# Clustered 1x1 convolution on one core: the order of the first three units, and squares summed by fp32 products

## The reference

```
xn  = x / |x| ;  cn = centroids / |centroids|       # over the channels
idx = argmax_n (xn . cn)                            # the nearest centroid of each place
mean[n] = mean of the x of all places whose idx is n    # the image's own centroids
delta = mean[idx] - x
alpha = exp(-mean over channels of delta^2)
y   = x + alpha * delta
out = relu(W y + bias)
```

## Time and profile before

| | us |
|---|---|
| median of 3 runs (lowest, highest) | 459.74 (459.32, 461.93) |
| the profiled execution | 459.06 |
| its span, first to last instruction | 457.3 |
| TensorE busy | 423.6 (93% of the span) |
| VectorE busy | 292.1 (64%) |
| ScalarE busy | 243.7 (53%) |
| GpSimd busy | 206.1 (45%) |

### The profile page before, as it was taken

The page is one execution under the profiler, slowest core; times in us unless marked ns, Lnnn a source line. Parts: engine busy times, 40 slices in busy tenths (PEclk is TensorE's granted clock), DMA queues, the critical chain, the costliest instruction groups (busy, mean ns, idle before and its releaser), DMA issues.

```text
span 457.3 us, 5730 instructions
## 1 busy us (share of the span) xinstructions
PE 423.6 (93%) x2100; PEld 294.1 (64%) x2100; DVE 292.1 (64%) x386; ACT 243.7 (53%) x330; POOL 206.1 (45%) x102
## 2 busy tenths in 40 slices
PE   4965677699999999999999999999999999999997
PEld 3722344367767775777676775777586776777785
DVE  2444697394767495676777486758578476577740
ACT  5452334354674566555565466455465467466542
POOL 2000047063582585384574476276556458233440
PEclk9996788989999999999999999999999999999999
DMA  8991046979756857487937966585928402221133
GB/s 285 287 224 46 1 92 143 225 212 249 190 179 174 195 195 176 140 239 174 267 100 186 241 177 189 132 235 148 259 93 207 163 7 87 92 80 54 52 127 149
DMA packets 70927, 73.94 MB, mean 162 GB/s; under 512 B 2724, under 2 KB 45732, under 8 KB 70900
## 3 DMA queue, kind: packets, MB, share of 16 engines
q1 hardware_dynamic: 70900, 73.58, 58.4%
HBM read 48.40 MB, written 25.17 MB: 161 GB/s over the span
## 4 chain that ended last, share of the span: by engine, by line
PE 89%; DVE 5%; issue 3%; ACT 1%; DMA 1%; SPq 0%; ACTq 0%; DVEq 0%
PE main L751 19%; PE main L753 19%; PE main L752 19%; PE fa L668 10%; PE sump L709 9%; PE gat L732 5%; PE al L739 1%; PE fa L692 1%; DMA x<-x 1%; PE al L740 1%; PE fa L677 1%; DVE z L361 1%; DVE z L341 1%; DVE xt L286 1%; PE main L762 1%
## 5 line engine op out<-in xcount | busy, mean ns | idle before, releaser
L256 POOL TENSOR_TENSOR z<-z,x 128x1024 f32<-128x1024 f32 x43 | 101.7, 2386 | 221.2 <-DVE z L361 221.2
L751 PE MATMUL main<-yh,wh 128*128 128x512 f32 x376 | 153.9, 409 | 2.1 <-ACT o L512 2.1
L753 PE MATMUL main<-yh,wl 128*128 128x512 f32 x376 | 147.8, 393 | 0.0
L752 PE MATMUL main<-yl,wh 128*128 128x512 f32 x376 | 147.6, 392 | 0.0
L341 DVE TENSOR_TENSOR z<-gat,x 128x1024 f32<-128x1024 f32 x47 | 57.4, 1221 | 93.4 <-PE gat L732 93.4
L512 ACT ACTIVATE o<-main,bcol 128x512 f32<-128x512 f32 x96 | 65.9, 687 | 85.8 <-PE main L753 85.8
L263 POOL TENSOR_TENSOR yl<-z,yh 128x1024 fp32r<-128x1024 f32 x43 | 103.0, 2410 | 12.1 <-ACT yh L504 12.1
L751 PEld LDWEIGHTS main<-yh,wh 128*128 128x128 f32 x376 | 71.0, 189 | 23.6 <-issue 4.6
L753 PEld LDWEIGHTS main<-yh,wl 128*128 128x128 f32 x376 | 71.0, 189 | 16.0
L752 PEld LDWEIGHTS main<-yl,wh 128*128 128x128 f32 x376 | 71.2, 189 | 14.7
L504 ACT ACTIVATE yh<-z 128x1024 fp32r<-128x1024 f32 x48 | 50.5, 1051 | 17.2 <-POOL z L256 16.0
(11 more groups left out here) (99 smaller groups left out, 321.7 us busy)
## 6 DMA issues: line engine op xcount, KB each, us to landing
x<-x SPq DMA_DIRECT2D x24, 1024.0 KB, 5.6
out<-o SPq DMA_DIRECT2D x23, 1024.0 KB, 4.7
xs<-x SPq DMA_DIRECT2D x84, 256.0 KB, 5.9
o<-w SPq DMA_DIRECT2D x1, 1024.0 KB, 12.1
out<-o SPq DMA_DIRECT2D x4, 256.0 KB, 2.0
sq<-centroids SPq DMA_DIRECT2D x2, 80.0 KB
bcol<-bias SPq DMA_DIRECT2D x1, 2.0 KB, 11.5
```

Source lines behind the costliest of these rows:

```text
L256: pool.tensor_tensor(z, z, X[g // PARTS % 2][:, pair(h), span(g)], ALU.add).then_inc(y_pool, 1)
L751: t_.matmul(main[:, o % 2, :], WH[:, k, rows], YH[g % 2][:, k, :], start=(k == 0), stop=False)
L752: t_.matmul(main[:, o % 2, :], WH[:, k, rows], YL[g % 2][:, k, :], start=False, stop=False)
L753: last = t_.matmul(main[:, o % 2, :], WL[:, k, rows], YH[g % 2][:, k, :], start=False, stop=(k == KC - 1))
```

## The change

Units 0 and 1 (DIRECT = 2) no longer add their squares on VectorE. ScalarE writes all four blocks of squares into the output tiles OUT[0] and OUT[1], which are free then, and `sum_squares_direct` sums them over blocks and partitions by four fp32 products with the matrix of ones, each 128 x 512 with 128 weight columns, into `al` (unit 0) or a bank of `gat` (unit 1). Both halves of y of unit 0 are made by VectorE, both low halves by GpSimd (before: half 0 of each by VectorE, half 1 by GpSimd). The second halves of the gathers of units 0 and 1 go to `main`. The means of image 0 lie in `al` instead of `fa`, so that the similarities of image 1 wait for the copied one-hot matrix and no longer for G. The lists ahead of the loop are reordered on TensorE, VectorE and ScalarE: among it, image 1's argmax comes right behind the four deltas of units 0 and 1, its cluster sums stand between the convolution steps of unit 0, and the similarities of units 1 and 2 follow each other. Unit 0's third output block is convolved in two pieces. SP loads x of unit 4 before the blocks of unit 3 and x of unit 5 before the blocks of unit 4. The loop is the same but for the counts in waits, and `relu(0, 3)`, which has moved ahead of it.

The diff without context lines, cut to its core:

```
@@ -33,0 +34,2 @@
+DIRECT = 2
@@ -40 +42,6 @@
...
@@ -40 +42,6 @@
-def on_vector(g, h):
+def y_on_vector(g, h):
+    return g == 0 or (g >= TAIL and h == 1)
+def low_on_vector(g, h):
@@ -42 +49 @@
-    return (g == 0 and h == 0) or (g >= TAIL and h == 1)
+    return g >= TAIL and h == 1
...
@@ -49,2 +57,4 @@
-def made_by_pool(g, h):
-    return 2 * g + h + 1 - made_by_vector(g, h)
+def folded(g):
+    return max(0, g + 1 - DIRECT)
@@ -116 +126,6 @@
-        mean = fa[0:NK, 0, :]
+        def mean(b):
+    return al[0:NK, :] if b == 0 else fa[0:NK, 0, :]
+        def alpha(g):
+    return gat[:, 0, :] if g == 1 else al[:, :]
@@ -157 +172,6 @@
-    return main if (g, h) == (0, 1) else gat
+    return main if g < DIRECT and h == 1 else gat
+        def squares(g, h):
+    if g < DIRECT:
+        return OUT[g][:, pair(h), :]
+    return SQ[:, :, :] if h == 0 else gat[:, :, :]
...
@@ -203,3 +225,6 @@
-    for g in range(PARTS, 2 * PARTS):
-        load_x(g)
-        load_xs(g)
+    load_x(3)
+    load_x(4)
+    load_xs(3)
+    load_x(5)
+    load_xs(4)
+    load_xs(5)
...
@@ -345 +370 @@
-        upper = banks(g, 1)
+        upper = squares(g, 1)
@@ -349 +374 @@
-        dve.wait_ge(pair_done, 2 * g + 2)
+        dve.wait_ge(pair_done, 2 * folded(g))
@@ -354 +379 @@
-        dve.wait_ge(sh_done, g + 1)
+        dve.wait_ge(sh_done, folded(g))
@@ -361 +386 @@
-        v_.tensor_tensor(z, z, al[:, :].unsqueeze(1).to_broadcast([P, 2, UNIT]), ALU.mult
+        v_.tensor_tensor(z, z, alpha(g).unsqueeze(1).to_broadcast([P, 2, UNIT]), ALU.mult
...
@@ -408,0 +434 @@
+    transpose_half(3, 0)
@@ -412,7 +438,5 @@
-    delta(0, 0)
-    delta(0, 1)
-    add_squares(0)
-    delta(1, 0)
-    low_sum(0)
-    delta(1, 1)
-    transpose_half(3, 0)
+    transpose_half(3, 1)
+    for g in range(DIRECT):
+        delta(g, 0)
+        delta(g, 1)
+    argmax(1)
@@ -422,9 +446 @@
-    add_squares(1)
-    low_half(0, 0)
-    low_sum(1)
-    transpose_half(3, 1)
-    argmax(1)
-    delta(2, 0)
-    scale(1, 0)
-    scale(1, 1)
-    delta(2, 1)
+    y_half(0, 1)
@@ -433 +449,2 @@
-    add_squares(2)
+    scale(1, 0)
+    scale(1, 1)
@@ -435 +451,0 @@
-    low_sum(2)
@@ -436,0 +453,2 @@
+    delta(2, 0)
+    delta(2, 1)
@@ -438,0 +457 @@
+    add_squares(2)
@@ -439,0 +459 @@
+    low_sum(2)
@@ -487,4 +507,7 @@
-        if h == 0:
-            wait(act, s_done, g)
-        a_.activation(SQ[:, :, :] if h == 0 else banks(g, 1)[:, :, :], Z[g % 2][:, pair(h), :], ACT.Square
-              ).then_inc(sq_done, 1)
+        if g < DIRECT:
+            act.wait_ge(wT_ps, KC)
+            act.wait_ge(const_done, 7)
+        elif h == 0:
+            wait(act, s_done, folded(g - 1))
+        a_.activation(squares(g, h), Z[g % 2][:, pair(h), :], ACT.Square).then_inc(sq_done, 1)
...
@@ -499 +522 @@
-        a_.activation(al[:, :], al[:, :], ACT.Exp, scale=-1.0 / C).then_inc(exp_done, 1)
+        a_.activation(alpha(g), alpha(g), ACT.Exp, scale=-1.0 / C).then_inc(exp_done, 1)
...
@@ -566 +592,0 @@
-    keep_transposed(1, 1)
@@ -567,0 +594 @@
+    keep_transposed(1, 1)
@@ -570,6 +597,5 @@
-    for k in range(KC):
-        act.wait_ge(wT_ps, k + 1)
-        a_.activation(WH[:, k, :], wT(k), ACT.Copy).then_inc(wh_done, 1)
-        if k == 0:
-            copy_onehot(0)
-    evacuate_onehot(0)
+    high_weights(0)
+    high_weights(1)
+    copy_onehot(0)
+    high_weights(2)
+    high_weights(3)
@@ -576,0 +603 @@
+    evacuate_onehot(0)
@@ -579 +605,0 @@
@@ -580,0 +607 @@
+    copy_sims(4)
@@ -581,0 +609 @@
+    copy_sims(5)
@@ -583,2 +610,0 @@
-    high_sum(0)
-    copy_sims(4)
@@ -586 +611,0 @@
-    exp(0)
@@ -588 +613,3 @@
-    copy_sims(5)
+    exp(0)
+    copy_onehot(1)
+    exp(1)
@@ -590 +616,0 @@
-    high_sum(1)
@@ -592,4 +617,0 @@
-    exp(1)
-    copy_onehot(1)
-    square(2, 0)
-    square(2, 1)
@@ -599 +620,0 @@
-    high_sum(2)
@@ -601,2 +622 @@
-    relu(0, 2)
-    evacuate_onehot(1)
+    square(2, 0)
@@ -603,0 +624,2 @@
+    square(2, 1)
+    evacuate_onehot(1)
@@ -604,0 +627,3 @@
+    high_sum(2)
+    relu(0, 2)
+    relu(0, 3)
@@ -609 +634,2 @@
-        relu(g - 3, 3)
+        if g > PARTS:
+            relu(g - 3, 3)
@@ -657 +683,3 @@
-        wait(pe, g_ready, b)
+        if b == 1:
+            pe.wait_ge(ohT_done, 1)
+        wait(pe, g_ready, b if b > 1 else 0)
...
-        pe.wait_ge(ohT_done, b + 1)
+        if b > 0:
+            pe.wait_ge(ohT_done, b + 1)
@@ -719,2 +748,2 @@
-        t_.matmul(mean, rows, sumsH[:, :], start=True, stop=False)
-        t_.matmul(mean, rows, sumsL[:, :], start=False, stop=True).then_inc(cop_done, 1)
+        t_.matmul(mean(b), rows, sumsH[:, :], start=True, stop=False)
+        t_.matmul(mean(b), rows, sumsL[:, :], start=False, stop=True).then_inc(cop_done, 1)
@@ -726,3 +755,5 @@
-        if h == 0:
-            wait(pe, s_done, g)
-        elif banks(g, h) is gat:
+        if g == 0:
+            pe.wait_ge(wl_done, KC)
+        elif g < DIRECT:
+            pe.wait_ge(z_done, 2 * (g - 1) + h + 1)
+        elif h == 1:
@@ -729,0 +761,5 @@
+        elif g == DIRECT:
+            pe.wait_ge(za_done, 2 * g)
+        else:
+            pe.wait_ge(s_done, folded(g - 1))
@@ -737,2 +773,2 @@
-        pe.wait_ge(sh_done, g + 1)
-        pe.wait_ge(sl_done, g + 1)
+        pe.wait_ge(sh_done, folded(g))
+        pe.wait_ge(sl_done, folded(g))
@@ -742,5 +778 @@
-    def convolve(g, o):
-        if not 0 <= g < UNITS:
-            return
-        wait(pe, relu_done, KC * g + o - 1)
-        rows = slice(o * P, (o + 1) * P)
+    def sum_squares_direct(g):
...
+            if k % 2 == 0:
+        pe.wait_ge(sq_done, 2 * g + k // 2 + 1)
+            last = t_.matmul(alpha(g), ones[:, :].bitcast(F32), OUT[g][:, k, :],
+             start=(k == 0), stop=(k == KC - 1))
+        last.then_inc(one_done, 1)
+    def convolve(g, o, ks=range(KC)):
+        if ks[0] == 0:
+            wait(pe, relu_done, KC * g + o - 1)
+        rows = slice(o * P, (o + 1) * P)
+        for k in ks:
@@ -755 +798,2 @@
-        last.then_inc(main_done, 1)
+        if ks[-1] == KC - 1:
+            last.then_inc(main_done, 1)
@@ -771,0 +816,14 @@
+    def transpose_weights(k):
+        pe.wait_ge(w_in, 16)
+        pe.wait_ge(xe_act, 3 if k < 2 else 4)
+        for o in range(KC):
+            last = t_.transpose(wT(k)[:, o * P:(o + 1) * P], Wraw[:, o, k * P:(k + 1) * P], ident[:, :])
+        last.then_inc(wT_ps, 1)
+    def high_passes(ks):
+        for o in range(2):
+            for k in ks:
+        for weights in (WH, WL):
+            t_.matmul(main[:, o, :], weights[:, k, o * P:(o + 1) * P], YH[0][:, k, :],
+              start=(k == 0 and weights is WH), stop=False)
@@ -775,0 +834 @@
+    similarities(2)
@@ -776,0 +836 @@
+    transpose_sims(0)
@@ -778 +837,0 @@
-    similarities(2)
@@ -780 +838,0 @@
-    transpose_sims(0)
@@ -782,6 +840,2 @@
-    pe.wait_ge(w_in, 16)
-    for k in range(KC):
-        pe.wait_ge(xe_act, 3 if k < 2 else 4)
-        for o in range(KC):
-            last = t_.transpose(wT(k)[:, o * P:(o + 1) * P], Wraw[:, o, k * P:(k + 1) * P], ident[:, :])
-        last.then_inc(wT_ps, 1)
+    transpose_weights(0)
+    transpose_weights(1)
@@ -790 +844,2 @@
-    transpose_onehot(0)
+    transpose_weights(2)
+    transpose_weights(3)
@@ -792,0 +848 @@
+    transpose_onehot(0)
@@ -795 +851,2 @@
-    pe.wait_ge(wl_done, KC)
+    similarities(3)
+    similarities(4)
@@ -798 +855 @@
-    similarities(3)
+    similarities(5)
@@ -801,3 +857,0 @@
-    similarities(4)
-    sum_squares(0)
-    similarities(5)
@@ -805,8 +859,3 @@
-    def high_passes(ks):
-        for o in range(2):
-            for k in ks:
-        for weights in (WH, WL):
-            t_.matmul(main[:, o, :], weights[:, k, o * P:(o + 1) * P], YH[0][:, k, :],
-              start=(k == 0 and weights is WH), stop=False)
+    sum_squares_direct(0)
+    sum_squares_direct(1)
+    sum_clusters(1, 0)
@@ -815,2 +863,0 @@
-    sum_squares(1)
-    gather(2, 0)
@@ -819 +866 @@
-    gather(2, 1)
+    sum_clusters(1, 1)
@@ -827,4 +874,3 @@
-    convolve(0, 2)
-    sum_squares(2)
-    for u in range(PARTS):
-        sum_clusters(1, u)
+    gather(2, 0)
+    sum_clusters(1, 2)
+    gather(2, 1)
@@ -832 +878 @@
-    convolve(0, 3)
+    convolve(0, 2, range(0, 2))
@@ -833,0 +880,3 @@
+    convolve(0, 2, range(2, KC))
+    convolve(0, 3)
+    sum_squares(2)
```

More of the change, by code:

```diff
@@ L325, in rest_of_mean @@
                 dve.wait_ge(mean_step, 2 * b + 2)
-                v_.scalar_tensor_tensor(out=mean, in0=part[:, :], scalar=below2[:, :], in1=mean,
+                v_.scalar_tensor_tensor(out=mean(b), in0=part[:, :], scalar=below2[:, :], in1=mean(b),
                                         op0=ALU.mult, op1=ALU.add).then_inc(rest_step, 1)
                 dve.wait_ge(rest_step, 2 * b + 1)
-                v_.tensor_copy(part[:, :], mean).then_inc(rest_step, 1)
+                v_.tensor_copy(part[:, :], mean(b)).then_inc(rest_step, 1)
             def parts_of_mean(b):
@@ L333, in parts_of_mean @@
```

(56 more changed lines are left out.)

66 lines of the change are left out of this document (27 added, 39 removed).

## The result

The changed kernel takes 435.56 us (median of 4 runs, 435.03 to 436.3), the kernel before 460.84 beside it: ratio 0.9449, 95% interval 0.9419 to 0.948. The forecast was 437.5 us, with a chance of 0.65 for 432.5 to 440. The profiled execution has a span of 433.4 us, TensorE busy 420.2 of them, and a mean granted clock of 1.00 (before 0.973).

What follows compares the result with a forecast made beforehand. TensorE was taken to bound the loop, so only an earlier loop start pays: 459.06 us, minus 20.2 for the start and 1.7 for the clock patch, gives 437.2, stated as 437.5 (432.5 to 440, chance 0.65).

Steps and rivals of the forecast that it cites:

- What bounds the kernel: TensorE fills the loop over units 3 to 23, busy 343.72 of 344.00 us; only an earlier loop start pays.
- Parts 1 and 2: Start to argmax 1: means scaled at 31.0 us, first gather 34.7, argmax 1 at 40.5, 21.9 us earlier.
- Part 3: Squares of units 0 and 1: eight fp32 products at 0.88 us make 7.0 us, mostly covered; 0.44 the lower bound.
- Part 4: Argmax 1 to the loop: GpSimd's chain decides; TensorE gap 2.8 us from 60.5; gather of unit 3 at 68.75.
- Part 5: Clock: 1.7 us charged behind TensorE's gap at 60.5, loop start 70.4; 1.76 us saved behind the old gap.
- low end: 432.5 us: 0.44 us products (0.8), no clock loss at 60.5 (1.7) and 2 for overlap not seen.
- (b): Rival: only the eight direct products meet the low clock, 7 us more up to unit 1's exponential; 444, chance 0.14.
- (a): Rival, slower: the lower clock stays before the loop, which starts at about 98 us; 466.5, chance 0.03.
- Part 6: Transfers: unit 5's x there by 33 us, wanted at 35.6; units 6 and 7 by 68; nothing on the path.
- (c): Rival: gain given back by handovers before the loop or unit 7's late x, 3 to 6 us; 441, 0.17 with (d).
- (d): Rival: unit 5's x lands late, so argmax 1 moves less; about 2 us at 38, 439; chance 0.17 with (c).

## Why the prediction was right, and where it was off

**What bounds the kernel** held: the loop stayed as dense as it was, and the gain is the earlier start and the slow patch at its beginning.

**Parts 1 and 2** came out within 0.2 us: scaling of the means at 31.01 (forecast 31.0), first gather 34.65 (34.7), first delta 35.67 (35.85), argmax 1 at 40.42 (40.5). Undoing the bank (7.2 us) and the load order (1.8 us) shows what they rest on. Argmax 1 at 40.42 is not itself what the gain hangs on: with it at 48.50 only 2.0 us are lost. What counts is that unit 0's y, and with it GpSimd, starts early.

**Part 3**, the price of a full-width fp32 product: eight records in 3.43 us (39.23 to 42.66), 0.86 us per product, the upper reading of the cluster sum's records and not the 0.44 us of their spacing. The rule of the Trainium skill (FP8 and Floating Point Precision, TensorE Precision Notes), four passes for true FP32, fits the trace: 0.86 us is 3.7 times the 0.23 us of a rounded product. What it was to cost was smaller still than reckoned: 0.8 us by the working, 0 by the run with rounded products, because GpSimd loses under VectorE's addition (0.50 us) what it wins by starting sooner (0.52 us).

**Part 4**: GpSimd's chain decides, as said (doubling one half moved the start by 2.37 us). Two of its sizes were off and cancel, which is luck: unit 0's high half starts at 46.79 instead of 47.25, and the two low halves last 5.33 us instead of 4.8, so GpSimd's first y half starts at 53.22 as against 53.1. The third did not cancel: ScalarE's one-hot copy is done at 62.83 instead of 63.3, since its operations overlap a little where they follow each other, and TensorE's gap is 2.0 us instead of 2.8. The start is at 68.11 against 68.75 before the clock's charge. That the distance from argmax 1 to G equals the old one was no argument, as the late argmax shows.

**Part 5** is the step that failed in size: 1.7 us were charged for a lower clock behind TensorE's gap, and none of the ten executions of the changed kernel shows it. It is most of what the forecast is too high by, 435.4 against a span of 433.4: 1.7 for the clock, 0.6 for part 4, less 0.3 in the loop's length. The forecast's low end took this in. Its high end is said to take in (b), but (b) at 444 lies outside the 440 beside it; the measurement is well under both. The rivals with a persistent low clock, (a) and (b), did not occur: TensorE had no idle time in the direct products, and the clock was 1.00. The kernel with VectorE's sums shows a clock of 0.50 from 45 to 57 us, so their mechanism is real in this stretch.

**Part 6** held for the new order; (c) and (d) did not occur.

## What to carry to other kernels

When a prologue is a chain over four engines, look for the idle time of the bottleneck engine and ask which buffer keeps ready work out of it: here one PSUM bank for the means, with the orders that it allows, was worth 7 us, and summing squares on the idle TensorE, at 0.86 us a product where a rounded one takes 0.23, up to 9. Such filler can count twice, as it also keeps up the engine's clock. Check too what an operation that waits holds back behind it in its engine's queue: that was 3 of the 9 us. To find which chain sets the end, double one operation on it: two distances that are equal before and after prove nothing.

## What the runs showed of the hardware

GpSimd's subtraction of two SBUF tiles (128 x 1024) lasts 2.36 us alone, 2.98 with 0.70 us of overlap with VectorE's addition of two SBUF tiles, and 3.48 with 1.22 us: about 0.9 us lost for each us of overlap, while the addition itself keeps its 1.23 us. The Trainium skill (SBUF — State Buffer, Who interferes with whom) says that a VectorE instruction with two SBUF inputs contends with a GpSimd instruction that reads SBUF; the rows agree. Here VectorE's addition had started first (47.19 and 47.69), and the loss is on GpSimd's side. In the kernel before it is the other way round:

```profile
57.24 2.38 POOL L256 TENSOR_TENSOR z<-z,x 128x1024 f32<-128x1024 f32 x1 [54.17 <-DVE z L361]
```

GpSimd keeps its 2.38 us there, and VectorE's subtraction that starts at 59.00, 0.62 us before GpSimd is done, lasts 1.70 us instead of the 1.23 of the same line alone.

The same kernel can keep its clock in one execution and lose it in another: with 3.4 us of idle at 61 us one of six had a mean clock of 1.00, the others 0.992 to 0.996. The length of this one gap does not tell the two apart: with 2.0 to 2.1 us of it the changed kernel had 1.00 ten times of ten, the one with cheap products 0.996 once in four.
